# Sums into the state ahead of the gate, two later units for the third norm's tokens, and both ends of the MoE part rearranged

## The chip, the cores and the metric
The kernel is one program on one core of one Trainium2 chip. The metric is the time of one execution on the device in microseconds (us). The kernel before has a median of 2390.23 us over three runs (2389.24 to 2395.43).

## The reference
Two layers with four layer norms over 16 sequences of 512 tokens of width 128, all in f32. `P` is 128, and the batch number is called i, j or b below.

```
x = norm(x + ssm(x))            # W_in, causal conv of 4 taps, pointwise product, silu; 8 states:
                                #   h = exp(delta*A)*h + delta*B*u;  y = sum over states of C*h
                                #   y = (y + xc*D) * silu(z);  y @ W_out
x = norm(x + x @ sign(W).T)
x = norm(x + attn(x))           # 16 heads of 64:  s = exp(g)*s + k^T v;  o = q s,  k gated by sigmoid
                                #   RMS norm of o, gate sigmoid(x @ Wog.T), @ Wo.T
x = norm(x + moe(x))            # logits x @ gate; top 2 of 8 experts, softmax of the two
                                #   silu(x @ w0[e]) * (x @ w1[e]) @ wo[e], mixed by the two weights
```

## The kernel before, in words
The work falls into three parts. First come **rounds** (`rounds`, L562, a hardware loop over round r from 3 to 15 with the first and last rounds written out). A round does three things at once for three different batches: the front of the state-space model for batch n, its eight states and first two norms for batch i, and the attention of batch j. A round has eight **units** u (`project(u, j)`: products q, g and k of one pair of heads) and then eight **stages** h (`stage(h, i, j, n)`: chunk c = h // 2 of 128 tokens, half f = h % 2 of the heads). The third norm and the routing of batch j - 1 (`closing(u, j - 1, j)`) lie between the units. The order of every engine is the order in which the code is written; engines meet only at semaphores.

PE writes into six PSUM banks used in turn (`ring_uses`, `Uses`); a product waits until the bank's last reader has drained it. In a stage PE does `update` (bank U, the chunk's sum for the state), `front(h + 1)` (v, the gates, the turned keys, two masks D and two score banks S), some of the state-space products, every second stage `project_out`, and last `outputs(h)`. With seven or nine uses in a stage, a late bank of `front(h + 1)` is the one that held U, so PE waits there for DVE's `add_update(h)` (L1603; L1605 in the first chunk). DVE's `gate_out(h - 1)` (L1561, L1565) reads the outputs of the stage before, once ACT has squared them (L1163). The scans of the states (L1448), the products with C (L1456, `ch`) and with B (L1441, `push`) also run on DVE, and POOL adds each `ch` to `y` by a DMA that accumulates (L1875). POOL also raises variances to the power -0.5 (L1880).

The second part is the **turn**: the last batch's choice of experts, the rows' places (`find_rows`, POOL), the store of the rows by indirect DMA (`send_rows`, L1944), the zero rows behind each expert's region (`pad_rows`, L664, SP), the table of tiles (DVE, L1759 to L1777), and the first loads of rows (L680). Then 136 tiles of 128 rows go through the experts (L1016, L1027), and their results are scattered.

The third part is the **final norm**: for each batch SP loads the two results of each token (`load_both`, L697), POOL adds the token (`add_token`, L2027), DVE adds the two (L1833) and takes the statistics, POOL makes scale and shift, ACT normalizes (L1358), and SP stores (L701).

Of the kernel before, what the change touches and what calls it, by code (L numbers as in the profile page):

```python
# [7 lines left out]
P = 128  # L8
T = 512
TILES = T // P  # L10
# [7 lines left out]
EXPERTS = 8  # L18
# [16 lines left out]
LN_STEPS = 11  # L35
RMS_EPS = float(np.finfo(np.float32).eps)
# [165 lines left out]
LATE = {0: [f"wo_{TILES - 1}"], 3: ["x3T"], 4: ["route"]}  # L202
# [7 lines left out]
FINAL_SLOTS = 4  # L210

# [4 lines left out]
PRODUCTS_IN_UNIT = {2: 1, 4: 2, 6: 3}  # L216
# [11 lines left out]
INDEX_STAGE = 0  # L228
SPREAD_AFTER = {4: (2, 3), 7: (4, 5, 6, 7)}

def build(nc, a, out):
# [6 lines left out]
    with ExitStack() as ctx:  # L238
# [32 lines left out]
        minus_half = sb_kept("minus_half", [P, TILES])  # L271
# [11 lines left out]
        def sem(name):  # L283
# [114 lines left out]
        both = sb_kept("both", [P, FINAL_SLOTS, 2, TILES, P])  # L398
# [11 lines left out]
        x3_dram = nc.dram_tensor("x3_scratch", [B, T, P], F32, kind="Internal").ap().rearrange(  # L410
            "b (c p) d -> b p c d", p=P)
# [104 lines left out]
        s_both = [sem(f"both_results_loaded{n}") for n in range(FINAL_SLOTS)]  # L516
# [24 lines left out]
        out_dram = out.rearrange("b (c p) d -> b p c d", p=P)  # L541
        both_dram = results_dram[0:2 * B * T, :].rearrange("(r b c p) d -> r b p c d", r=2, b=B, p=P)
# [14 lines left out]
        HOT_STEPS, ROW_STEPS, SHARE_STEPS = 13, 14, 5  # L557
        STAGES = 2 * TILES
# [3 lines left out]
        def rounds(eng, body):  # L562
# [7 lines left out]
            body(None, B - 1, None)  # L570

# [7 lines left out]
        def _(sp):  # L579
# [93 lines left out]
            def load_rows(i):  # L673
                for n in range(2):
# [4 lines left out]
                    for c in range(MOE_LOAD):  # L679
                        sp.dma_start(rows_in[:, n, c, :], rows_dram[rows_at(g * MOE_LOAD + c), :]).then_inc(s_rows_in[n], 16)  # L680

            def load_tokens(b):
                sp.dma_start(tokens[:, bass.ds(b * TILES, TILES), :],
                             x3_dram[bass.ds(b, 1)].rearrange("b p c d -> (b p) c d")).then_inc(s_tokens, 16)
# [10 lines left out]
            def load_both(b):  # L695
                for r in range(2):
                    sp.dma_start(both[:, b % FINAL_SLOTS, r, :, :], both_dram[r, b]).then_inc(s_both[b % FINAL_SLOTS], 16)  # L697

# [1414 lines left out]
```

## Time and profile before
| | us |
|---|---|
| median of three runs | 2390.23 |
| the profiled execution, its own time | 2394.66 |
| its span | 2392.8 |
| PE busy in the span | 2069.4 (86%) |
| DVE busy | 1955.2 (82%) |
| ACT busy | 1411.5 (59%) |
| POOL busy | 838.3 (35%) |

The busy shares are averages over the three parts. The profile's slices show PE at 0.8 to 1.0 through the rounds and through the tiles, and at 0 in the last 60 us. The chain that ended last is PE for 50% of the span, DVE for 21%, issue for 12% and ACT for 9%. A row of a timeline gives the start in us, the length, the engine, the line and what it writes and reads; in brackets stands how long the engine was idle before, and what it waited for.

### The profile page before, as it was taken

The page shows a single profiled execution, that of the slowest core. Times are in us where ns is not written, and L with a number is a line of the kernel's source. Part 1 is how long each engine was busy: PE and PEld are TensorE (multiplying, and loading weights), DVE is VectorE, ACT ScalarE, POOL GpSimd, SP SyncE. Part 2 cuts the span into 40 slices and gives each one's busy share as a digit, 9 for nine tenths or more (in the row PEclk, how much of TensorE's full clock was granted, in tenths as well). Part 3 has the DMA queues.
Part 4 walks back from the last instruction along what each step waited for, and adds up shares of the span by engine and source line. Part 5 has one row for each costly group of instructions (what it writes and reads, how often), then busy time and mean ns, then how long its engine had stood idle before and what let it go on. Part 6 is the DMA issues. An engine that isn't in the chain of part 4 may idle for free.

```text
span 2392.8 us, 52303 instructions
## 1 busy us (share of the span) xinstructions
PE 2069.4 (86%) x15736; PEld 1543.1 (64%) x15865; DVE 1955.2 (82%) x3681; ACT 1411.5 (59%) x3240; POOL 838.3 (35%) x1060
## 2 busy tenths in 40 slices
PE   4589999998999898989898999989989569999980
PEld 2256666665656575756565665656676569999980
DVE  6788989889898989898989898888985457777768
ACT  3466676666766667676676666666656323333334
POOL 0011515152524343342514151515243233333337
PEclk7699999999999999999999999999999889999995
DMA  6352424334242434242515243333421232212216
GB/s 179 89 116 59 116 72 106 88 84 105 67 106 67 118 81 111 72 110 64 124 49 127 62 115 77 95 97 75 102 67 35 76 104 59 58 55 62 60 57 191
DMA packets 154382, 212.88 MB, mean 89 GB/s; under 512 B 20296, under 2 KB 88912, under 8 KB 153920
## 3 DMA queue, kind: packets, MB, share of 16 engines
q1 hardware_dynamic: 132048, 144.20, 20.5%
q0 software_dynamic: 22272, 67.92, 13.8%
q8 instruction: 31, 0.51, 0.1%
q14 instruction: 31, 0.25, 0.0%
HBM read 134.71 MB, written 28.08 MB: 68 GB/s over the span
## 4 chain that ended last, share of the span: by engine, by line
PE 50%; DVE 21%; issue 12%; ACT 9%; DMA 4%; POOL 1%; DVEq 1%; SPq 0%; ACTq 0%; POOLq 0%
PE banks L1016 8%; PE banks L1027 4%; PE banks L911 4%; PE banks L889 3%; PE banks L884 3%; DVE ch L1456 3%; PE banks L859 3%; PE banks L750 3%; PE banks L838 3%; PE banks L854 3%; PE banks L807 3%; DVE hs L1448 2%; DVE push L1441 2%; DMA y<-ch 2%; ACT S L1195 2%
## 5 line engine op out<-in xcount | busy, mean ns | idle before, releaser
L1448 DVE TENSOR_TENSOR_SCAN hs<-decay,push 128x512 f32<-128x512 f32 x256 | 312.9, 1244 | 4.9
L1195 ACT ACTIVATE S<-banks,fall_tok 128x128 f32<-128x128 f32 x1024 | 277.7, 384 | 27.3 <-PE banks L826 27.1
L1016 PE MATMUL banks<-rowsT,w_here 128*128 128x128 f32 x2176 | 269.2, 277 | 6.9 <-DVE w_here L1795 6.8
L1016 PEld LDWEIGHTS banks<-rowsT,w_here 128*128 128x128 f32 x2176 | 255.6, 193 | 10.5 <-issue 9.3
L1875 POOL DMA_DIRECT2D y<-ch x96 | 88.0, 917 | 451.2 <-DVE ch L1456 349.3
L1966 POOL TENSOR_TENSOR qd<-q,q_fall 128x512 f32<-128x512 f32 x96 | 157.9, 1645 | 239.5 <-ACT chunk_fall L1180 239.4
L2009 POOL DMA_INDIRECT results_scratch<-rows_out,result_to x136 | 131.9, 970 | 241.1 <-ACT rows_out L1323 234.3
L1554 DVE TENSOR_TENSOR S<-banks,S 128x512 f32<-128x512 f32 x256 | 166.5, 681 | 45.0 <-PE banks L838 26.7
L1441 DVE TENSOR_TENSOR push<-du,b_all 128x1024 f32<-128x1024 f32 x128 | 198.0, 1547 | 4.6 <-DMA b_all<-bc_scratch 4.6
L1312 ACT ACTIVATE tanh_h<-banks 128x512 f32<-128x512 f32 x136 | 81.3, 598 | 203.4 <-PE banks L1016 203.4
L838 PE MATMUL banks<-q,k 64*128 64x128 f32 x1024 | 152.0, 290 | 51.2 <-DVE state L1603 37.2
L1944 POOL DMA_INDIRECT rows_scratch<-x,row_now x128 | 172.0, 1344 | 40.2 <-issue 36.6
L1106 ACT ACTIVATE decay<-delta,a_neg 128x512 f32<-128x512 f32 x256 | 172.0, 730 | 20.2 <-DVE hs L1448 19.4
L1561 DVE SCALAR_TENSOR_TENSOR oT<-tog,banks 128x512 f32<-128x512 f32 x128 | 87.3, 682 | 106.1 <-ACT sq L1163 105.6
L807 PE MATMUL banks<-x2T,w_k 128*128 128x512 f32 x256 | 134.0, 605 | 45.5 <-DVE k L1547 45.5
L838 PEld LDWEIGHTS banks<-q,k 64*128 64x128 f32 x1024 | 127.5, 193 | 66.1 <-DVE state L1603 31.8
L1456 DVE TENSOR_TENSOR ch<-hs,c_all 128x1024 f32<-128x1024 f32 x128 | 159.9, 1249 | 3.1 <-DMA y<-ch 1.0
L1880 POOL TENSOR_TENSOR rstd<-var,minus_half 128x4 f32<-128x4 f32 x48 | 48.7, 1014 | 297.9 <-DVE var L1422 297.9
L839 PE MATMUL banks<-q,k 64*128 64x128 f32 x1024 | 152.5, 291 | 0.0
L911 PEld LDWEIGHTS banks<-w_o,oT 128*128 128x128 f32 x1024 | 123.6, 193 | 35.6 <-issue 33.5
L1163 ACT ACTIVATE sq<-banks 128x512 f32<-128x512 f32 x128 | 76.9, 601 | 116.3 <-PE banks L889 116.3
L1027 PE MATMUL banks<-w,act_h 128*128 x1088 | 143.6, 275 | 0.4 <-DVE act_h L1787 0.4
(218 smaller groups left out, 5139.2 us busy)
## 6 DMA issues: line engine op xcount, KB each, us to landing
y<-ch POOLq DMA_DIRECT2D x96, 512.0 KB, 5.4
b_all<-bc_scratch SPq DMA_DIRECT2D x128, 256.0 KB, 3.8
c_all<-bc_scratch SPq DMA_DIRECT2D x128, 256.0 KB, 3.6
q_fall<-fall_scratch SPq DMA_DIRECT2D x192, 128.0 KB, 3.3
rows_in<-rows_scratch SPq DMA_DIRECT2D x136, 66.0 KB
both<-results_scratch SPq DMA_DIRECT2D x32, 256.0 KB, 3.4
w<-w_dram SPq DMA_DIRECT2D x3, 2048.0 KB, 8.8
xT<-xT_dram SPq DMA_DIRECT2D x16, 256.0 KB, 2.9
```

The lines of the kernel that those rows point to most:

```text
L807: pe.matmul(bank, w[:, u * P:(u + 1) * P], x2T[:], start=True, stop=True).then_inc(full, 1)
L838: even = pe.matmul(low[:, at_h], k[0:DH, pair, here], q[0:DH, pair, here], start=True, stop=True)
L911: pe.matmul(bank[:, 0:P], oT[:, t, :], w_o[:, t, :], start=(t == 0), stop=(t == PAIRS - 1))
L1016: mm = pe.matmul(bank_h[:, u % 2, n, here], w_here[:, u % 2, n, here], x, start=True, stop=True)
L1027: mm = pe.matmul(bank_y[:, u % 2, 0:P], act_h[:, u % 4, f * P:(f + 1) * P], w_2[:, bass.ds(e * FF + f * P, P)], start=(f == 0), stop=(f == ...
L1106: nc.scalar.activation(decay[:, n % 2, h, :], delta[:, h, :], ACT.Exp, scale=a_neg[:, h, n:n + 1]).then_inc(s_decay, 1)
L1195: ins = nc.scalar.activation(S[:, g, here], bank[:, here], ACT.Exp, bias=fall_tok[:, head:head + 1])
L1441: nc.vector.tensor_tensor(push[:], du[:], b_all[:, slot, :].unsqueeze(1).broadcast_to([P, HALVES, T]), ALU.mult).then_inc(s_push, 1)
L1448: nc.vector.tensor_tensor_scan(hs[:, h, :], decay[:, n % 2, h, :], push[:, h, :], 0.0, ALU.mult, ALU.add).then_inc(s_scan, 1)
L1456: nc.vector.tensor_tensor(ch[:, n % 2, :, :], hs[:], c_all[:, slot, :].unsqueeze(1).broadcast_to([P, HALVES, T]), ALU.mult).then_inc(s_ch, 1)
L1554: nc.vector.tensor_tensor(S[:, g, :], full(ring, f"S{g}_{c}", j), S[:, g, :], ALU.mult).then_inc(ring.free_sem(f"S{g}_{c}"), 1)
L1944: nc.gpsimd.indirect_dma_start(out=rows_dram, out_offset=bass.IndirectOffsetOnAxis(ap=row_now[:, n, t:t + 1], axis=0), in_=x3_rows[:, t, : ...
```

## The change
It has four pieces.

1. In every stage from the third on, DVE adds the chunk's sum to the state (`add_update`) ahead of `gate_out`.
2. In the units, the products of state 1 (`ch` of state 1 and `push` of state 2) go from unit 2 to unit 1, those of state 2 from unit 4 to unit 3. PE turns the third norm's tokens in unit 4 instead of 3 and takes the logits in unit 5 instead of 4; DVE chooses the experts in unit 6, behind the seventh key, instead of in unit 5.
3. At the turn, the last batch's places are found on DVE (`find_last_rows`) in nine counted steps; the zero rows are split between SP and ACT; the row numbers of the first four tiles are read before the wait for the scattered rows; and the first weights are copied before the first rows are awaited.
4. In the final norm, tokens, results and output move with four consecutive tokens per partition (2 KB in one piece instead of four pieces of 512 bytes); `both` has eight slots instead of four; DVE adds the token, POOL no longer does; mean, variance, scale and shift are made for two batches at a time; and ACT issues the stores.

```diff
-LATE = {0: [f"wo_{TILES - 1}"], 3: ["x3T"], 4: ["route"]}
+LATE = {0: [f"wo_{TILES - 1}"], 4: ["x3T"], 5: ["route"]}
-PRODUCTS_IN_UNIT = {2: 1, 4: 2, 6: 3}
+PRODUCTS_IN_UNIT = {1: 1, 3: 2, 6: 3}
+CHOOSE_UNIT = 6
+BOTH_SLOTS = 8
@@ layouts
+        tokens_dram = x3_scratch.rearrange("b (p c) d -> b p c d", p=P)
-        out_dram = out.rearrange("b (c p) d -> b p c d", p=P)
-        both_dram = results_dram[0:2 * B * T, :].rearrange("(r b c p) d -> r b p c d", r=2, b=B, p=P)
+        out_dram = out.rearrange("b (p c) d -> b p c d", p=P)
+        both_dram = results_dram[0:2 * B * T, :].rearrange("(r b p c) d -> r b p c d", r=2, b=B, p=P)
@@ SP, turn
-            for e in range(EXPERTS):
-                pad = bass.ds(sp.value_load(pad_row[0:1, e:e + 1], min_val=0, max_val=ALL_ROWS - P), P)
-                sp.dma_start(rows_dram[pad, :], a["pad_rows"][e * P:(e + 1) * P, :]).then_inc(s_spared, 16)
+            clear_pads(sp, range(EXPERTS // 2))
             sp.wait_ge(s_tile_row, 1)
+            first_rows = [bass.ds(sp.value_load(row_i[0:1, c:c + 1], min_val=0, max_val=ALL_ROWS - P), P)
+                          for c in range(MOE_LOAD)]
             sp.wait_ge(s_spared, 16 * (EXPERTS + 1))
             sp.wait_ge(s_scattered, 16 * 2 * TOK_TILES)
@@ SP, end
-            for b in range(FINAL_SLOTS):
-                load_both(b)
             for b in range(B):
-                store(b, b % FINAL_SLOTS)
-                if b + FINAL_SLOTS < B:
-                    sp.wait_ge(s_mixed, b + 1)
-                    load_both(b + FINAL_SLOTS)
+                after(sp, s_mixed, b - BOTH_SLOTS + 1)
+                load_both(b)
@@ PE and ACT, closing: the two blocks move from u == 3 and u == 4
+                if u == 4:
+                    pe.wait_ge(s_x3, at(j, TILES, TILES))
...
+                if u == 5:
+                    bank, full = fill(ring, "route", it, "x3T")
@@ ACT
+            act.wait_ge(s_pads, 1)
+            clear_pads(act, range(EXPERTS // 2, EXPERTS))
...
+            def store(b):
+                n = b % FINAL_SLOTS
+                act.wait_ge(s_final, TILES * (b + 1))
+                act.dma_start(out_dram[b], final[:, n]).then_inc(s_out[n], 16)
             for b in range(B):
                 normalize_final(b)
+                if b:
+                    store(b - 1)
+            store(B - 1)
@@ DVE, stage
                 if j is not None:
-                    if h == 1:
-                        add_update(h, j)
+                    add_update(h, j)
                     if h:
                         gate_out(h - 1, j)
-                    if h != 1:
-                        add_update(h, j)
@@ DVE, turn
+            def find_last_rows(j):
...
+                for t in range(TILES):
+                    step(nc.vector.tensor_tensor(next_row[:, t + 1, :], next_row[:, t, :], ranks[:, 1, t, :], ALU.add))
+                nc.vector.tensor_copy(pad_row[:], done[0:1, :]).then_inc(s_pads, 1)
+                step(nc.vector.tensor_tensor(ranks[:, 0], ranks[:, 0], next_row[:, 0:TILES, :], ALU.add))
+                for n in range(2):
+                    step(nc.vector.tensor_tensor(rows_f[:], ranks[:, 0], hot[:, n], ALU.mult))
+                    step(nc.vector.tensor_reduce(row_f32[:, n, :], rows_f[:], AX.X, ALU.add))
@@ DVE, first tile
+            weights_here(0, 0)
             rows_to(0, 0)
@@ DVE, end
-            for b in range(B):
-                mix_results(b)
-                final_deviation(b)
+            dve.wait_ge(s_tokens, 16 * B)
+            for m in range(B // 2):
+                for step in (mix_results, add_token, final_stats):
+                    for b in (2 * m, 2 * m + 1):
+                        step(b)
+                final_deviation(m)
@@ POOL, body: sum_state(m, i) stands ahead of closing(u, ...), in the units of PRODUCTS_IN_UNIT
@@ POOL, end: add_token is gone
-            for b in range(B):
-                final_shift(b)
+            for m in range(B // 2):
+                final_shift(m)
```

The first place is DVE's row between the deviation of the third norm (`x3`, in unit 1) and the key of unit 3, in the loop. `hs` is the scan, `ch` and `push` the products of the states, `k` a key, `fall` the running sum of the decay. Before:

```order
L1547 SCALAR_TENSOR_TENSOR k<-tg,banks 128x512
L1429 TENSOR_SCALAR x3<-x3,mean,rstd 128x128 x4
L1526 SCALAR_TENSOR_TENSOR sp_in<-sp_in,sp_ln 112x512
L1533 SCALAR_TENSOR_TENSOR fall<-ones,sp_in 112x128 x4
L1456 TENSOR_TENSOR ch<-hs,c_all 128x1024
L1441 TENSOR_TENSOR push<-du,b_all 128x1024
L1448 SCALAR_TENSOR_TENSOR hs<-decay,push 128x512
L1448 SCALAR_TENSOR_TENSOR hs<-decay,push 128x512
L1547 SCALAR_TENSOR_TENSOR k<-tg,banks 128x512
```

Now:

```order
L1476 TENSOR_TENSOR ch<-hs,c_all 128x1024
L1461 TENSOR_TENSOR push<-du,b_all 128x1024
L1567 SCALAR_TENSOR_TENSOR k<-tg,banks 128x512
L1449 TENSOR_SCALAR x3<-x3,mean,rstd 128x128 x4
L1546 SCALAR_TENSOR_TENSOR sp_in<-sp_in,sp_ln 112x512
L1553 SCALAR_TENSOR_TENSOR fall<-ones,sp_in 112x128 x4
L1468 SCALAR_TENSOR_TENSOR hs<-decay,push 128x512
L1468 SCALAR_TENSOR_TENSOR hs<-decay,push 128x512
L1567 SCALAR_TENSOR_TENSOR k<-tg,banks 128x512
```

The products of state 1 and the push of state 2 stand before the key and the normalizing of `x3`, where they stood behind the decay's sums; the scan of state 2 no longer follows its push directly.

On POOL, at the same place, `rms` and `rstd` belong to the third norm and `y<-ch` is the accumulating DMA of a state. Before:

```order
L1886 TENSOR_TENSOR rms<-mixed,rms_eps 128x1
L1889 TENSOR_TENSOR rms<-rms,minus_half 128x1
L1880 TENSOR_TENSOR rstd<-var,minus_half 128x4
L1875 DMA y<-ch 128x1024
L1875 DMA y<-ch 128x1024
L1875 DMA y<-ch 128x1024
```

Now:

```order
L1941 TENSOR_TENSOR rms<-mixed,rms_eps 128x1
L1944 TENSOR_TENSOR rms<-rms,minus_halves 128x1
L1930 DMA y<-ch 128x1024
L1935 TENSOR_TENSOR rstd<-var,minus_halves 128x4
L1930 DMA y<-ch 128x1024
L1930 DMA y<-ch 128x1024
```

The DMA of state 1 is issued ahead of the norm's power, where it came behind it.

On DVE in stage 2, `oT` and `sq_less` are the gate of stage 1's outputs and `state` the chunk's sum. Before:

```order
L1481 SCALAR_TENSOR_TENSOR xc<-th,xc 128x512
L1561 SCALAR_TENSOR_TENSOR oT<-tog,banks 128x512
L1565 TENSOR_TENSOR sq_less<-sq 128x256
L1603 TENSOR_TENSOR state<-state,banks 64x4x64 x2
L1448 SCALAR_TENSOR_TENSOR hs<-decay,push 128x512
L1587 TENSOR_TENSOR kd<-banks,to_end 128x512
```

Now:

```order
L1501 SCALAR_TENSOR_TENSOR xc<-th,xc 128x512
L1623 TENSOR_TENSOR state<-state,banks 64x4x64 x2
L1581 SCALAR_TENSOR_TENSOR oT<-tog,banks 128x512
L1585 TENSOR_TENSOR sq_less<-sq 128x256
L1468 SCALAR_TENSOR_TENSOR hs<-decay,push 128x512
L1607 TENSOR_TENSOR kd<-banks,to_end 128x512
```

The two halves of the sum stand ahead of the two instructions of the gate; nothing is added.

## Rows read from the trace of the kernel before

**Rows 1.** Windows view of one middle round: stretch, busy us per engine, clock, DMA.
```profile
1008.87:1121.62 112.75, 102.96 (x770) 71.21 (x778) 98.77 (x178) 77.02 (x180) 41.82 (x50) 1.00 0.37 90
```

**Rows 2.** Line L1113 over the whole span: durations in ns, first and last start.
```profile
L1113 ACT COPY x2T<-banks x16: 585/586/586, 103.0 to 1796.1; 128x512 f32<-128x512 f32 x16
```

**Rows 3.** Waits of PE, whole span: who waited for whom, us, times, longest.
```profile
PE banks L807 <- DVE k L1547: 45.5, 29, 2.7
PE banks L838 <- DVE state L1603: 37.2, 16, 4.6
...
PE banks L956 <- DVE x L1429: 20.3, 16, 5.7
...
PE banks L743 <- DVE state L1603: 6.8, 14, 0.5
```

**Rows 4.** Timeline of DVE, projections of that round: start us, length, then idle before.
```profile
1022.86 0.69 DVE L1547 SCALAR_TENSOR_TENSOR k<-tg,banks 128x512 f32<-128x512 f32 x1 [0.69 <-ACT tg L1141]
1023.46 1.11 DVE L1429 TENSOR_SCALAR x<-x,mean,rstd 128x128 f32<-128x128 f32 x4
...
1026.66 1.20 DVE L1456 TENSOR_TENSOR ch<-hs,c_all 128x1024 f32<-128x1024 f32 x1
1027.77 1.22 DVE L1441 TENSOR_TENSOR push<-du,b_all 128x1024 f32<-128x1024 f32 x1
1029.12 2.34 DVE L1448 TENSOR_TENSOR_SCAN hs<-decay,push 128x512 f32<-128x512 f32 x2
```

**Rows 5.** Timeline of POOL, the same stretch.
```profile
1022.24 1.02 POOL L1880 TENSOR_TENSOR rstd<-var,minus_half 128x4 f32<-128x4 f32 x1 [4.95 <-DVE var L1422]
1028.45 0.92 POOL L1875 DMA_DIRECT2D y<-ch  x1 [5.20 <-DVE ch L1456]
```

**Rows 6.** Timeline of DVE in stage 2 of that round.
```profile
1066.37 0.67 DVE L1561 SCALAR_TENSOR_TENSOR oT<-tog,banks 128x512 f32<-128x512 f32 x1
...
1067.31 0.86 DVE L1603 TENSOR_TENSOR state<-state,banks 64x256 f32<-64x256 f32 x2
```

**Rows 7.** Timeline of PE in stage 2, the row that waits.
```profile
1068.22 0.37 PE L838 MATMUL banks<-q,k 64*128 64x128 f32 x1 [2.28 <-DVE state L1603]
```

**Rows 8.** Timeline of ACT in stage 4, the row that starts its long chain.
```profile
1096.27 0.69 ACT L1090 ACTIVATE delta<-banks,b_dt 128x512 f32<-128x512 f32 x1 [1.56 <-PE banks L769]
```

**Rows 9.** Line L1944 at the turn, 1895 to 1930 us.
```profile
L1944 POOL DMA_INDIRECT rows_scratch<-x,row_now x8: 954/978/1855, 1910.5 to 1920.5; - x8
```

**Rows 10.** Line L1699 at the turn, 1895 to 1910 us.
```profile
L1699 DVE TENSOR_TENSOR hot<-hot,rev x2: 191/192/192, 1900.7 to 1902.1; 128x32 f32<-128x32 f32 x2
```

**Rows 11.** Timeline of all engines from the last ranks to the first expert product.
```profile
1903.71 1.03 POOL L1909 TENSOR_TENSOR next_row<-next_row,ranks 128x8 f32<-128x8 f32 x4 [8.84 <-ACT ranks L1259]
...
1923.86 8.49 SPq L680 DMA_DIRECT2D rows_in<-rows_scratch  x8
...
1929.63 0.16 DVE L1801 TENSOR_TENSOR is_best<-rows_in,expert_place 128x4 f32<-128x4 f32 x1 [11.51 <-DMA rows_in<-rows_scratch]
...
1930.84 0.58 ACT L1306 COPY rowsT<-banks 128x512 f32<-128x512 f32 x1 [27.19 <-PE banks L1002]
...
1932.78 1.62 PE L1016 MATMUL banks<-rowsT,w_here 128*128 128x128 f32 x6 [2.05 <-DVE w_here L1795]
```

**Rows 12.** Line L1833, the final sum on DVE, whole span.
```profile
L1833 DVE TENSOR_TENSOR final_in<-both x16: 683/692/694, 2332.5 to 2384.4; 128x512 f32<-128x512 f32 x16
```

**Rows 13.** Timeline of all engines in the final norm.
```profile
2334.63 1.28 POOL L2027 TENSOR_TENSOR both<-both,tokens 128x512 f32<-128x512 f32 x1 [2.15 <-DMA both<-results_scratch]
...
2368.89 1.23 DVE L1844 TENSOR_TENSOR var<-stats 128x4 f32<-128x4 f32 x1
...
2371.24 0.87 DVE L1839 BATCH_NORM_STATS2 stats<-final_in 128x6 f32<-128x128 f32 x4
...
2388.34 1.65 ACT L1358 ACTIVATE final<-final_in,shift,rstd 128x128 f32<-128x128 f32 x4 [0.41 <-POOL shift L2036]
```

**Rows 14.** Windows view, ten us in the middle of the final norm.
```profile
2355.00:2365.00 10.00, 0.00 (x0) 0.00 (x0) 9.59 (x36) 4.94 (x12) 8.12 (x8) 0.50 0.80 224
```

More of the change, by code:

```diff
@@ L397, in build @@
         rows_out = sb_kept("rows_out", [P, 2, MOE_LOAD, P])
-        both = sb_kept("both", [P, FINAL_SLOTS, 2, TILES, P])
+        both = sb_kept("both", [P, BOTH_SLOTS, 2, TILES, P])
         stats4 = sb_kept("stats4", [P, FINAL_SLOTS, TILES, 6])
@@ L515, in build @@
         s_results = [sem("results_stored0"), sem("results_stored1")]
-        s_both = [sem(f"both_results_loaded{n}") for n in range(FINAL_SLOTS)]
+        s_both = [sem(f"both_results_loaded{n}") for n in range(BOTH_SLOTS)]
         s_mixed = sem("results_mixed")
@@ L557, in build, with last @@
         HOT_STEPS, ROW_STEPS, SHARE_STEPS = 13, 14, 5
+        LAST_ROW_STEPS = 9
+        def last(j):
+            return isinstance(j, int) and j == B - 1
         STAGES = 2 * TILES
@@ L570, in rounds, with clear_pads @@
             body(None, B - 1, None)
+        def clear_pads(eng, some):
+            for e in some:
+                pad = bass.ds(eng.value_load(pad_row[0:1, e:e + 1], min_val=0, max_val=ALL_ROWS - P), P)
+                eng.dma_start(rows_dram[pad, :], a["pad_rows"][e * P:(e + 1) * P, :]).then_inc(s_spared, 16)
         def attention_over(eng):
@@ L1725, in body @@
                             fall_less(FALL_PARTS.index(u), j)
+                        if u == CHOOSE_UNIT and not first(j):
+                            choose(j - 1, j)
                     if i is not None and u in PRODUCTS_IN_UNIT:
@@ L1740, in _, with step @@
                 closing(u, B - 1, END)
+                if u == CHOOSE_UNIT:
+                    choose(B - 1, END)
+            attention_over(dve)
+            done = next_row[:, TILES, :]
+            def find_last_rows(j):
+                steps = [0]
+                def step(ins):
+                    steps[0] += 1
+                    ins.then_inc(s_route, 1)
+                    dve.wait_ge(s_route, at(j, ROW_STEPS, steps[0]))
+                drained(dve, ring, END, "rank")
+                dve.wait_ge(s_route, at(j, ROW_STEPS, 0))
+                dve.wait_ge(s_row_now, at(j, 3, 0))
+                for t in range(TILES):
[5 more added lines that the diff above has]
+                    step(nc.vector.tensor_reduce(row_f32[:, n, :], rows_f[:], AX.X, ALU.add))
+                assert steps[0] == LAST_ROW_STEPS
+            find_last_rows(B - 1)
             index_rows(B - 1)
-            attention_over(dve)
-            dve.wait_ge(s_route, ROW_STEPS * B)
-            done = next_row[:, TILES, :]
-            nc.vector.tensor_copy(pad_row[:], done[0:1, :]).then_inc(s_pads, 1)
             steps = [0]
@@ L1811, in experts @@
                     t = i * MOE_BODY + u
-                    weights_here(t, u)
+                    if u or not first(i):
+                        weights_here(t, u)
                     if u == MOE_LOAD - 1:
@@ L1938, in send_rows @@
                     pool.wait_ge(s_share, at(j, SHARE_STEPS, SHARE_STEPS))
-                    nc.gpsimd.tensor_tensor(next_row[:, 0, :], next_row[:, TILES - 1, :], ranks[:, 1, TILES - 1, :],
-                                            ALU.add).then_inc(s_route, 1)
+                    if not last(j):
+                        nc.gpsimd.tensor_tensor(next_row[:, 0, :], next_row[:, TILES - 1, :], ranks[:, 1, TILES - 1, :],
+                                                ALU.add).then_inc(s_route, 1)
                 for k in SCATTERS[u]:
@@ L1953, in closing @@
                 if u == RANK:
-                    find_rows(j, it)
+                    if not last(j):
+                        find_rows(j, it)
                     shares(j)
```

88 lines of the change are left out of this document (41 added, 47 removed).

## The prediction
> **What bounds the kernel now.** I read the page first: span, shares, slices and the chain that ended last. PE is on that chain for half of it, so the next view is who PE waits for; then one middle round of the timeline, engine by engine; last the turn from the rounds to the experts and the final norm, where PE is idle. The reader is to see four things.
>
> A round takes (1796.1 - 103.0) / 15 = 112.9 us [rows 2]. In the one I followed PE is busy for 102.96 of 112.75 us and DVE for 98.77 [rows 1]: neither is full, they take turns in waiting. PE's waits are for DVE nearly all: for a key's bank 45.5 us in all, for the chunk's sum 37.2 us in 16 waits (and 6.8 us at another bank), for the third norm's tokens 20.3 us in 16 [rows 3]. The round's clock is 1.00, the upper of TensorE's two levels (2.4 GHz) [rows 1], so those waits don't lower it. At the turn PE does nothing from the last ranks to 1929.63. In the final norm DVE is busy for 9.59 of 10 us [rows 14], but 1.23 us of that is an instruction on 128x4 elements that lay beside POOL's token sum [rows 13]; an instruction of that size beside an idle POOL takes 0.16 [rows 11].
>
> **Sums ahead of the gate.** Nothing is added; two DVE instructions of the gate go behind two of the sum. In stage 2 the gate starts at 1066.37 and the sum at 1067.31 [rows 6], so the sum comes 0.94 us earlier. PE stood idle for 2.28 us for it [rows 7], so it gets the whole 0.94. The table has 16 such waits of 2.3 us on average [rows 3], one to a round: 16 x 0.94 = 15.0 us. The gate is now 0.86 us later. Who waits for it: `project_out`, which PE reaches only behind a convolution or the mix, and ACT's gates in the stages where a new pair of chunks begins; I cost that at nothing, and if the cover were missing it would cost up to the 0.86 in one stage of each round.
> The 6.8 us at the other bank, in stage 5, will go too, but I count nothing for them: by then the round hangs on ACT. ACT's step sizes start when PE's L769 is done (1.56 us idle before, [rows 8]) and run through exp and log into the masks that DVE needs, and the next round's `push` follows from there. L769 lies behind stage 2 and ahead of stage 5, so the 0.94 us passes through it and the 0.5 us doesn't. Bounds: 0 (given back at another wait) and 15.0 + 6.8 = 21.8.
>
> **The units.** PE's wait for the third norm's tokens (about 0.95 us a round) goes, as it asks a unit later. That is worth nothing by itself: PE next waits for the keys anyway [rows 3], and those hang on DVE's row. So I count DVE's stalls. Before, the key of unit 2 had 0.69 us of idle time ahead of it, and the normalizing followed at once [rows 4]. Now ch of state 1 starts at about 1022.1, where the deviation ends, and takes 1.20. POOL must issue its DMA before the power: in [rows 4, 5] the DMA starts 0.59 behind the end of ch and takes 0.92, and the power takes 1.02; 1022.1 + 1.2 + 0.6 + 0.9 + 1.0 = 1025.8. DVE meanwhile has ch, push and the key (1.11, 1.22 and 0.60 by the starts and lengths of [rows 4]), done at 1025.0: a new stall of 0.8 in place of 0.69. Against it, a push is no longer followed at once by the scan that reads it, which cost 0.13 of idle each (1027.77 + 1.22 to 1029.12, [rows 4]), twice a round, and the second split of the decay no longer waits for ACT's cast, an estimate of 0.15 by the same kind of gap. Sum -0.8 + 0.69 + 0.4 = 0.3 us a round, 14 rounds: 4.2 us. Bounds: a gain of 1.2 a round if the power isn't delayed at all (17), and a loss of 1.0 a round (14), if the power is stretched beside push as far as that line's neighbours are, 1.0 and more.
> The choice of experts does the same work one key later; nothing waits for it before PE's ranks, behind front(0).
>
> **The turn.** POOL begins the places at 1903.71 [rows 11] and the first scatter starts at 1910.5 [rows 9], 6.8 us later. Now DVE takes ten counted or plain small steps of 0.225 (six of them in 1902.1 - 1900.7, [rows 10]), then three small instructions (0.36, two of them without a wait) and the scatter's own start (0.3, estimates both), and POOL's shares run beside it: scatter at 2.9 us. Gain 3.9; the eight scatters keep their ten us. The zero rows start at about 1904.7 on two queues and are out of the way. Behind the scatters SP reads a row number ahead of each load: eight loads in 8.49 us, 1.06 apart; the first four rows have landed 5.77 us after the first issue [rows 11]. With the numbers read before, the issues are, as an estimate, 0.43 apart: 3 x 0.63 = 1.9 us less. The first product started 1.36 us behind the turned rows (1930.84 + 0.58 to 1932.78), held by the weights' copy; with that copy ahead, 0.1: gain 1.2. Sum 7.0. Bounds 3 (the scatters' landing or the 2 MB weight loads hold it) and 9.
>
> **The final norm.** DVE's period is (2384.4 - 2332.5) / 15 = 3.46 us a batch [rows 12]. Without the stretched instruction (1.23 to 0.16, [rows 13]) a deviation is 3.46 - 0.72 - 0.87 - 1.07 = 0.8. A pair is now four sums of 0.69, two statistics of 0.87, one deviation of 0.8 and 0.1 of gaps: 5.4 us in place of 6.92. ACT has 2 x 1.65 [rows 13] and two stores to issue, 0.4 each as an estimate, 4.1 a pair, and keeps up, but a pair's second sum waits for the batch four before, and that loop (4.5 on DVE, 2.3 on POOL, 3.8 on ACT for two pairs) gives 5.3: just covered. The start: pair 0 needs the second batch, landed at 2334.63 before [rows 13], in longer pieces perhaps 2333.0; DVE is done with it at 2337.7, with the last pair at 2375.5. Then power and shift on eight columns 2.0, ACT 1.65 + 0.4 + 1.65, two stores, and the 2.8 us from ACT's end (2388.34 + 1.65) to the span's: 2384.4. Gain 8.4. Bounds 4 (loads as slow as before, the loop 0.4 longer) and 11.
>
> In this stage the DMA moved 224 GB/s at a share of 0.80 [rows 14], 280 GB/s when full; a pair moves 1.57 MB, which is 5.6 us at that rate, about DVE's 5.4. The Trainium skill (DMA: Bandwidth & Descriptors, Specifications) says that transfers from 512 bytes up already run at line rate. By that rule the longer pieces bring nothing, the pair would take 5.6 and the second batch would land as before: the end would gain 8.4 - 1.4 - 1.6 = 5.4, and the total below would be 31.6 in place of 34.6. No row here shows the same stream in 2 KB pieces, so this stays open; the range holds both.
>
> **Sum.** 15.0 + 4.2 + 7.0 + 8.4 = 34.6 us. The profiled execution has 2394.66 us, 1.9 more than its span and 4.4 more than the median: 2394.66 - 34.6 = 2360.1 for one like it, and 2390.23 - 34.6 = 2355.6 against the median. I say 2355.
>
> **Rivals.**
> - Only the ends gain. For it: PE waits 45.5 us for keys [rows 3], and what it gains at the sum's bank can be given back there, since DVE's own row in stage 2 gets no shorter. Against it: the start of ACT's chain follows PE. 2390.2 - 15.4 = 2374.8.
> - The rounds gain more: the power isn't delayed (17), the other bank's 6.8 us count as well: 21.8 + 17 + 15.4 = 54: 2336.
> - Slower: POOL's DMA in front of the power. It waits for ch of state 1 and for the start of the sum, so the normalizing of x3, behind it the decay, the scan of state 2 and every key after it stand still, on DVE, which has 14 us to spare in a round. It decides when the new stall exceeds 0.8 + 34.6 / 14 = 3.3 us a round. At 5 us it costs 14 x 4.2 = 59: 2390.2 - 34.6 + 59 = 2414. Against it: the 0.92 and 1.02 us of [rows 5].
> - Ends and rounds cancel: each round loses about 1 us, the bound above: 2390.2 - 15.4 + 14 = 2389.
> - The change doesn't do what it says: it is described as bringing state 1's product a unit later, but the table moves it from unit 2 to unit 1, earlier, and DVE's row shows this. The sums above go by the row, so no chance of its own.
>
> **How the numbers follow.** Forecast 0.52, only the ends 0.22, more in the rounds 0.15, cancelled 0.06, slower 0.05. What this kernel's measurement can tell from no change is about 0.3%, 7 us: below 2383 is faster. Faster 0.52 + 0.22 + 0.15 = 0.89, same 0.06, slower 0.05. The range leaves out the last two and the far end of the third case: 2332 to 2377. The forecast's own is 2345 to 2365.
>
> **What would show it.** The distance between x2T copies falls from 112.9 to about 111.6. PE's wait for L838 at the chunk's sum falls from 2.3 to about 1.4 us each, the one at the turned x1 goes to 0, and that for the third norm's tokens vanishes; a new wait of DVE appears at the normalizing of x3, for the power, near 0.8 us. The first scatter starts 2.9 us behind the ranks, the first product 3.8 + 1.9 us behind the first row load's issue. The last stage has one deviation per 5.4 us and ends 8 us sooner. I am wrong if the round's length doesn't fall (the key waits grow by what the sum's waits lose), if the stall at x3 is over 2 us, or if the two-batch loop through ACT, not DVE, sets the final norm at 6 us or more.

## The result, and the profile after

The changed kernel has a median of 2362.35 us over four runs (2360.64 to 2369.59), the kernel before 2392.83 over four; the ratio of the two is 0.9876, with a 95% interval of 0.9844 to 0.9907. The prediction was 2355 us, range 2332 to 2377. The profiled execution took 2363.93 us, span 2362.1: 30.7 us less than the one before, where the terms summed to 34.6. The total is close; two of its four terms are not, and they have opposite signs. One of the six executions of the kernel with the power first (experiment 2) took 5701.25 us; it counts in that kernel's median of 2344.79, but not in its ratio.

First the rounds. This is the line that copies x2T, once a round:

```profile
L1122 ACT COPY x2T<-banks x16: 586/586/586, 106.1 to 1785.1; 128x512 f32<-128x512 f32 x16
```

From the first to the last that is 1679.0 us in place of 1693.1 [rows 2]: 111.9 a round, 0.94 less, where 1.24 were predicted. The first copy comes 3.1 us later (106.1 for 103.0); in the twelve kernels of the experiments it lies between 102.8 and 106.2, whether they have the change or not, so I take that as scatter. The next view is the windows view of whole rounds (stretch, its length, busy us and instructions of PE, PE's weight loads, DVE, ACT, POOL, then PE's clock, DMA share, GB/s). The clock's column is the granted clock as a share of full speed. Two rounds of the kernel before, and five us inside the second:

```profile
1008.90:1121.60 112.70, 102.96 (x770) 71.21 (x778) 98.72 (x178) 76.97 (x179) 41.82 (x50) 1.00 0.37 90
1121.60:1235.90 114.30, 104.49 (x770) 71.79 (x778) 99.38 (x178) 77.07 (x181) 41.03 (x50) 0.99 0.36 91
1181.60:1186.60 5.00, 5.00 (x19) 2.31 (x18) 4.97 (x7) 1.36 (x3) 4.39 (x4) 0.66 0.12 41
```

Two rounds of the changed kernel, and six us inside the second:

```profile
776.20:887.90 111.70, 102.97 (x770) 71.02 (x778) 98.00 (x177) 76.92 (x180) 41.85 (x50) 1.00 0.38 92
1001.20:1114.30 113.10, 106.00 (x770) 72.84 (x778) 98.33 (x177) 77.17 (x180) 41.07 (x50) 0.97 0.34 89
1025.20:1031.20 6.00, 6.00 (x14) 3.39 (x13) 6.00 (x8) 4.20 (x8) 0.92 (x1) 0.50 0.71 187
```

The column of the clock is what the prediction missed. In both kernels there are rounds at 1.00 and rounds in which the clock falls to the lower of its two levels (0.50) for some us, and those are longer on average. Over the 13 rounds from the second copy to the fifteenth:

| | rounds with a fall | where | us a round at full clock | us with a fall | all 13 |
|---|---|---|---|---|---|
| before | 6 | 60 us in, stage 2 | 112.9 | 114.2 | 1475.2 |
| changed | 10 | 24 us in, units | 111.2 | 112.9 | 1462.7 |

What PE did before each fall stands in its timeline. Before, in the units and stage 2 of the second round; the last is the wait of [rows 7], a round later:

```profile
1144.97 1.12 PE L807 MATMUL banks<-x2T,w_k 128*128 128x512 f32 x2 [1.62 <-DVE k L1547]
...
1152.26 1.12 PE L807 MATMUL banks<-x2T,w_k 128*128 128x512 f32 x2 [1.47 <-DVE k L1547]
...
1181.09 0.37 PE L838 MATMUL banks<-q,k 64*128 64x128 f32 x1 [2.27 <-DVE state L1603]
```

In the changed kernel, units and stage 2 of the second round:

```profile
1019.79 0.66 PE L965 MATMUL banks<-eye,x 128*128 128x128 f32 x4 [0.87 <-DVE x L1449]
1024.77 1.67 PE L816 MATMUL banks<-x2T,w_k 128*128 128x512 f32 x2 [2.61 <-DVE k L1567]
...
1061.79 0.34 PE L847 MATMUL banks<-q,k 64*128 64x128 f32 x1 [1.52 <-DVE state L1623]
```

The wait for the chunk's sum is 1.52 in place of 2.27, and the clock no longer falls behind it. But PE stands idle for 2.61 us in one piece for the key of unit 3, where it had 1.62 and 1.47 in two pieces 7 us apart, and now the clock falls there. The matmuls behind it show it: a projection of two matmuls takes 1.67 to 2.05 us in place of 1.02. The Trainium skill (TensorE: Matmul & The Clock Gate, A second HAM failure mode: psum-queue depth-cycling) tells of a kernel in which short idle pieces of PE between groups of matmuls made its clock swing between the two levels. The trace agrees in so far as the clock falls here in 10 of 13 rounds, though PE is busy for 106.00 of the 113.1 us of the round shown; but here the falls stand behind one long piece and not behind many short ones.

PE's waits, 212.1 to 1674.8 us (who waited for whom, us, times, longest); these answer to [rows 3], which are of the whole span:

```profile
PE banks L816 <- DVE k L1567: 37.5, 22, 2.6
...
PE banks L965 <- DVE x L1449: 11.0, 13, 0.9
```

DVE's row in the units, to be held against [rows 4]:

```profile
1014.78 1.23 DVE L1476 TENSOR_TENSOR ch<-hs,c_all 128x1024 f32<-128x1024 f32 x1
...
1017.06 0.68 DVE L1567 SCALAR_TENSOR_TENSOR k<-tg,banks 128x512 f32<-128x512 f32 x1
1018.62 1.11 DVE L1449 TENSOR_SCALAR x<-x,mean,rstd 128x128 f32<-128x128 f32 x4 [0.88 <-POOL rstd L1935]
...
1021.83 2.31 DVE L1468 TENSOR_TENSOR_SCAN hs<-decay,push 128x512 f32<-128x512 f32 x2
1024.06 0.66 DVE L1567 SCALAR_TENSOR_TENSOR k<-tg,banks 128x512 f32<-128x512 f32 x1
```

and POOL's, against [rows 5]:

```profile
1016.60 0.91 POOL L1930 DMA_DIRECT2D y<-ch  x1 [6.60 <-DVE ch L1476]
1017.26 1.33 POOL L1935 TENSOR_TENSOR rstd<-var,minus_halves 128x4 f32<-128x4 f32 x1
```

POOL issues state 1's DMA ahead of the power, DVE waits 0.88 us for the power (0.8 was predicted), and the scan of state 2 comes before the next key: from one key to the next 7.0 us. In stage 2 DVE's order is the planned one, against [rows 6]:

```profile
1060.78 0.86 DVE L1623 TENSOR_TENSOR state<-state,banks 64x256 f32<-64x256 f32 x2
1061.67 0.69 DVE L1581 SCALAR_TENSOR_TENSOR oT<-tog,banks 128x512 f32<-128x512 f32 x1
```

Then the turn, against [rows 9] and [rows 11]:

```profile
1892.98 0.78 DVE L1777 TENSOR_TENSOR next_row<-next_row,ranks 128x8 f32<-128x8 f32 x4 [0.70 <-ACT ranks L1268]
...
1895.81 1.07 POOL L2000 DMA_INDIRECT rows_scratch<-x,row_now  x1 [0.80 <-DVE x L1690]
...
1908.91 6.70 SPq L697 DMA_DIRECT2D rows_in<-rows_scratch  x8
...
1912.38 0.16 DVE L1840 TENSOR_TENSOR is_best<-rows_in,expert_place 128x4 f32<-128x4 f32 x1 [3.57 <-DMA rows_in<-rows_scratch]
...
1914.25 2.08 PE L1025 MATMUL banks<-rowsT,w_here 128*128 128x128 f32 x8 [0.68 <-ACT rowsT L1318]
```

First scatter 2.8 us behind the start of the places (6.8 before; 2.9 predicted), first rows used 3.5 us behind the first load's issue (5.8; 3.8 predicted), first product 1.9 us behind that (3.15; 1.9 predicted). And the final norm, against [rows 12] and [rows 13]:

```profile
L1874 DVE TENSOR_TENSOR final_in<-both x16: 684/692/693, 2311.2 to 2349.9; 128x512 f32<-128x512 f32 x16
```

and the second sum of one pair of batches and of the next:

```profile
2329.10 0.69 DVE L1874 TENSOR_TENSOR final_in<-both 128x512 f32<-128x512 f32 x1 [0.19 <-ACT final L1370]
...
2334.30 0.69 DVE L1874 TENSOR_TENSOR final_in<-both 128x512 f32<-128x512 f32 x1 [0.20 <-ACT final L1370]
```

A pair takes 5.2 us (2334.3 - 2329.10; 5.4 predicted), the first load to the span's end 54.3 us in place of 65.4.

### The profile page after: what moved, and what is told of

Its sections match the earlier page's. It is cut to its first block and busy times, and to the rows that moved or that the text cites. A ratio compares the mean times of both kernels' runs of the same rounds, so it can differ in the third digit from the quotient of the medians.

```text
span 2362.1 us, 52250 instructions
## 1 busy us (share of the span) xinstructions
PE 2090.2 (88%) x15736; PEld 1555.9 (66%) x15865; DVE 1930.9 (82%) x3650; ACT 1411.8 (60%) x3240; POOL 810.2 (34%) x1014
## 3 DMA queue, kind: packets, MB, share of 16 engines
q1 hardware_dynamic: 105040, 139.73, 19.9%
## 5 line engine op out<-in xcount | busy, mean ns | idle before, releaser
L847 PE MATMUL banks<-q,k 64*128 64x128 f32 x1024 | 147.3, 284 | 39.3 <-DVE state L1623 25.2
L816 PE MATMUL banks<-x2T,w_k 128*128 128x512 f32 x256 | 142.9, 641 | 42.3 <-DVE k L1567 42.2
L848 PE MATMUL banks<-q,k 64*128 64x128 f32 x1024 | 147.9, 285 | 0.0
L816 PE MATMUL banks<-x2T,w_q 128*128 128x512 f32 x256 | 144.8, 649 | 0.0
L863 PE MATMUL banks<-w_v,x2T 128*128 128x512 f32 x256 | 143.3, 641 | 0.0
```

Of the source, the lines that this page charges most:

```text
L816: pe.matmul(bank, w[:, u * P:(u + 1) * P], x2T[:], start=True, stop=True).then_inc(full, 1)
L847: even = pe.matmul(low[:, at_h], k[0:DH, pair, here], q[0:DH, pair, here], start=True, stop=True)
```

## Experiments

Each of these kernels was timed beside the kernel before, in 4 to 12 executions, and its ratio is to those. Rounds, falls and waits are read from one profiled execution of each. Theory P is the prediction: every term is a sum of work and of waits. Theory C, formed after the result, adds the clock: it falls behind a stretch in which PE does little, and a change is also worth what it does to those stretches.

### 1. The four pieces, each alone

Each is the kernel before with one of the four numbered pieces of the change and nothing else. The whole edit of the first, and the core of the second:

```diff
                 if j is not None:
-                    if h == 1:
-                        add_update(h, j)
+                    add_update(h, j)
                     if h:
                         gate_out(h - 1, j)
-                    if h != 1:
-                        add_update(h, j)
```

```diff
-LATE = {0: [f"wo_{TILES - 1}"], 3: ["x3T"], 4: ["route"]}
+LATE = {0: [f"wo_{TILES - 1}"], 4: ["x3T"], 5: ["route"]}
-PRODUCTS_IN_UNIT = {2: 1, 4: 2, 6: 3}
+PRODUCTS_IN_UNIT = {1: 1, 3: 2, 6: 3}
+CHOOSE_UNIT = 6
```

> The kernel before with only the chunk's sums put ahead of the gate. Theory P (the prediction's terms): each round 0.94 us shorter, 15 to 16 us in all, ratio 0.9935. Theory C (the granted clock counts as well): PE's wait of 2.3 us in stage 2 falls to 1.4, so the clock no longer falls 58 to 66 us into a round, as it did in 6 of 13 middle rounds of the kernel before (114.1 us with the fall, 112.7 without), and the two copies' waits add up: the middle rounds take 111 to 111.3 us, all at 1.00; 13 x 2.3 = 30 us, ratio 0.987. Rival N: what is gained at the sum is given back at the keys; ratio 1.000, and the wait for keys grows from 40 us.

> The kernel before with only the units changed (products of states 1 and 2 a unit earlier, x3 turned in unit 4, logits in 5, choice behind the seventh key). Theory P: 4 us faster, ratio 0.998. Theory C: DVE waits 0.9 us for POOL's power ahead of the normalizing of x3, PE then waits 2.6 us in one piece for the key of unit 3, and the clock falls 22 to 32 us into the round in most rounds; the first state copy comes 41.2 us into the round in place of 38.7. Middle rounds 114.5 to 116 us, slower by 10 to 25 us, ratio 1.004 to 1.010. Rival N: same within 0.1%.

> The kernel before with only the final norm changed (four tokens per partition, eight slots, sums on DVE, two batches a deviation, stores by ACT). Theory P: 8.4 us faster, ratio 0.9965. By the trace of the changed kernel, where the first load of both results to the span's end took 54.3 us in place of 65.4: 11.1 us faster, ratio 0.9954. Rival: the gain there came from an earlier landing that this kernel does not have; under 5 us.

> The kernel before with only the turn changed (places on DVE in nine steps, zero rows on two queues, row numbers read ahead, first weights copied ahead). Theory P: 7.0 us faster, ratio 0.997. By the trace of the changed kernel, where last ranks to the first load of both results took 8.8 us less: ratio 0.9963. Rival: the tiles are held by the weight loads and give it back; under 2 us.

| alone | median us | ratio, interval | us by the ratio | predicted |
|---|---|---|---|---|
| sums | 2366.93 | 0.9886 (0.9870 to 0.9903) | -27 | -15.0 |
| units | 2421.32 | 1.0111 (1.0094 to 1.0128) | +27 | -4.2 |
| final norm | 2385.78 | 0.9961 (0.9943 to 0.9978) | -9 | -8.4 |
| turn | 2383.03 | 0.9959 (0.9945 to 0.9972) | -10 | -7.0 |

Theory C has the signs of the first two and nearly their sizes: 0.987 and 1.004 to 1.010 were expected. It had not expected the second fall with the units alone. A round with the sums alone, and PE's wait for the chunk's sum in it:

```profile
992.60:1104.10 111.50, 103.13 (x778) 71.18 (x778) 98.52 (x177) 76.90 (x179) 41.85 (x50) 1.00 0.37 94
```

```profile
1051.59 0.37 PE L838 MATMUL banks<-q,k 64*128 64x128 f32 x1 [1.34 <-DVE state L1603]
```

A round with the units alone, and its two falls:

```profile
1023.80:1139.60 115.80, 107.86 (x778) 73.87 (x778) 99.34 (x178) 77.30 (x180) 40.17 (x50) 0.96 0.34 89
1046.00:1054.00 8.00, 7.08 (x15) 3.88 (x16) 7.76 (x10) 5.38 (x11) 0.92 (x1) 0.60 0.63 158
1082.00:1096.00 14.00, 11.54 (x87) 8.55 (x87) 11.77 (x14) 6.71 (x19) 9.29 (x8) 0.88 0.50 124
```

and what PE waited for ahead of them:

```profile
1046.92 1.42 PE L808 MATMUL banks<-x2T,w_k 128*128 128x512 f32 x2 [2.61 <-DVE k L1548]
...
1084.87 0.34 PE L839 MATMUL banks<-q,k 64*128 64x128 f32 x1 [2.46 <-DVE state L1604]
```

With the sums alone the 13 rounds take 1447.2 us, and the clock fell in one of them, behind a wait of 2.08 us for the third norm's tokens. With the units alone they take 1502.3, and the clock fell twice in every one: behind 2.6 us of waiting for the key and behind 2.5 for the sum. The two parts of the ends were as predicted. The product of the four ratios is 0.992, not 0.988: the units cost less where the sums are also early. In the changed kernel no second fall is left in the 13 rounds, which fits.

The granted clock averaged over a whole execution is known for every one that was timed, and it goes the same way: 0.953 to 0.961 before, 0.946 to 0.950 changed, 0.959 to 0.960 with the sums alone, 0.934 to 0.938 with the units alone, 0.963 to 0.965 in the kernel with the old units below. So the falls are not a matter of the profiled executions only.

### 2. The units taken back, and POOL's power put first

The first is the changed kernel with the units as before (the second diff above backwards). The second changes POOL's body only:

```diff
-                    if m is not None:
+                    if m is not None and u != 1:
                         sum_state(m, i)
                     if j is not None:
                         if not first(j):
                             closing(u, j - 1, j)
+                    if m is not None and u == 1:
+                        sum_state(m, i)
```

> The changed kernel with the units as before (products of states 1 and 2 in units 2 and 4, x3 turned in unit 3, logits in 4, choice ahead of the seventh key). Theory C: middle rounds as with the sums alone, 111.2 us at 1.00, 16 us less than the changed kernel; ratio to before 0.981. Theory P: the units' 4 us are lost; ratio 0.989. Rival: the three gains overlap; 0.987.

> The changed kernel with POOL's power for x3 put ahead of the accumulating DMA of state 1 in unit 1. Theory C: DVE's wait of 0.9 us ahead of the normalizing of x3 goes, PE's wait for the key of unit 3 falls from 2.6 to 1.7 us in one piece, the clock stays at 1.00 in the units, and the middle rounds take 110.4 to 111.2 us in place of 112.5: 17 to 27 us less than the changed kernel, ratio to before 0.977 to 0.981. Theory P (no effect of the clock): 0.9 us a round at most, 12 us, ratio 0.983. Rival: PE gets the wait back at the next key; ratio 0.987 as the changed kernel.

Old units: 2346.58 us, ratio 0.9804 (0.9784 to 0.9824); all 13 rounds at 1.00, 111.4 us each, 1447.9 in all. So the new units cost the changed kernel 0.9876 - 0.9804, some 17 us; 14.8 of it lies in these 13 rounds. The product of the other three ratios is 0.981, so those gains add up. Between rounds at full clock they are worth next to nothing (111.2, of only three such rounds, to 111.4): the loss goes with the falls of the clock.

Power first: 2344.79 us, ratio 0.9786 (0.9764 to 0.9808), as expected in its size but not in its way. DVE's waits for the power, in the 13 rounds of the changed kernel:

```profile
DVE x L1449 <- POOL rstd L1935: 26.3, 26, 1.1
```

and of this one:

```profile
DVE x L1449 <- POOL rstd L1935: 14.7, 13, 1.1
```

The 0.9 a round went, and so did PE's wait for x3. PE's wait for the key did not shrink: PE came to it as much earlier as DVE did, and here is what is left of it:

```profile
PE banks L816 <- DVE k L1567: 36.2, 17, 2.6
```

The pieces are still of 2.6 us, and the clock still fell in 12 of 13 rounds. What came was 11.1 us in the 13 rounds (1451.6), near the stall of 0.88 times 13. But two more rounds had a fall, and the one round without took 109.5 us, 1.8 less than such rounds of the changed kernel, so that agreement is in part chance. In the profiled executions the last x2T copy comes 19.9 us earlier, at 1765.2: 3.3 us of it stand before the first copy and 5.4 behind the fifteenth, where the changed kernel's clock fell twice and this one's once.

### 3. More work for PE

The same matmuls are done three times over, so that PE reaches its long wait later; nothing else changes:

```diff
-                    for t in range(TILES):
+                    for t in 3 * list(range(TILES)):
                         mm = pe.transpose(bank[:, t * P:(t + 1) * P], x3[:, t, :], eye[:])
```

> The changed kernel with more work on PE: the four transposes of x3 are done three times over into the same bank, about 1.0 us more of PE ahead of its wait for the key of unit 3. If the fall of the clock follows from the piece of 2.6 us in which PE is idle, that piece shrinks to about 1.6 us, the clock stays at 1.00 and the kernel with more work is faster: middle rounds 111.2 to 111.8 us, 10 to 17 us less than the changed kernel, ratio 0.981 to 0.983. If it does not, the rounds are as long as in the changed kernel or up to 1 us longer: ratio 0.987 to 0.993.

> The changed kernel with POOL's power first and the four transposes of x3 done three times over: 1.0 us more of PE work ahead of its longest wait. Theory C: the piece in which PE is idle falls from 2.6 to 1.6 us, the clock falls in few rounds, middle rounds 109.5 to 110.8 us, 11 to 28 us less than with the power alone; ratio 0.967 to 0.974. Without an effect of the clock: 0.9786 or up to 0.984.

PE in the units of a round with the extra work alone, then that round and one with a fall:

```profile
1125.92 1.53 PE L965 MATMUL banks<-eye,x 128*128 128x128 f32 x12 [0.88 <-DVE x L1449]
1130.91 1.12 PE L816 MATMUL banks<-x2T,w_k 128*128 128x512 f32 x2 [1.74 <-DVE k L1567]
```

```profile
1107.20:1218.20 111.00, 103.84 (x778) 71.89 (x786) 98.09 (x178) 76.79 (x180) 41.84 (x50) 1.00 0.37 93
546.40:659.40 113.00, 106.85 (x778) 73.66 (x786) 98.98 (x178) 77.07 (x180) 41.04 (x50) 0.97 0.36 92
```

The changed kernel with 0.9 us more work a round is faster: 2350.60 us, ratio 0.9806 (0.9784 to 0.9828), against 0.9876 (0.9844 to 0.9907) without it. The kernel of experiment 5, which has the changed kernel's rounds and was timed beside this one, has 0.9877. Its wait is 1.74 in place of 2.61, and the clock fell in 6 of 13 rounds in place of 10. With the power first as well it is 2333.17 us, ratio 0.9747 (0.9729 to 0.9766), the fastest of all kernels here, though short of the 0.967 to 0.974 expected; the 13 rounds take 1438.3, and 9 of them were at 1.00. No sum of work and waits gives that sign: the wait is shorter by just the work that was added. It is an experiment and no good way to write a kernel: real work should stand there.

### 4. Real work or another order in its place

```diff
-SCANS_IN_UNIT = {1: 1, 3: 2, 5: 3}
-PRODUCTS_IN_UNIT = {1: 1, 3: 2, 6: 3}
+SCANS_IN_UNIT = {1: 1, 4: 2, 6: 3}
+PRODUCTS_IN_UNIT = {1: 1, 4: 2, 6: 3}
```

with the power first (even keys); the same with the products of state 3 in unit 7; and the even keys with the logits in unit 6 and the choice in unit 7.

> The changed kernel with POOL's power first, and state 2's scan and products moved from unit 3 to unit 4 and state 3's scan from unit 5 to 6, so that DVE's keys of units 3, 4 and 5 stand 3 to 4 us apart (5.4 and 2.9 between the keys of units 2, 3 and 4 with the power alone). Theory C: no piece of PE's wait for a key exceeds 1.7 us, the clock stays at 1.00 in the units and the middle rounds take 109.5 to 110.5 us, 15 to 28 us less than with the power alone; ratio to before 0.967 to 0.973. Theory P (only DVE's and PE's sums of work and waits count): as with the power alone, 0.9786. Rival: DVE's later scans delay the states in the stages by up to 2 us a round; 0.98 to 0.99.

> As the kernel with the keys evenly apart, and state 3's products in unit 7 in place of 6, behind the last key. Theory C: the last key comes 2.4 us earlier; if PE waits for it, rounds up to 1 us shorter than with the even keys alone, and POOL's accumulating DMA of state 3 comes at the same time as before; ratio 0.963 to 0.973. Rival: same as with the even keys, within 0.1%.

> As the kernel with the even keys (POOL's power first, scans of states 2 and 3 in units 4 and 6, products of state 2 in unit 4), where PE waited 2.1 us in one piece ahead of the logits for ACT's copy of the turned x3 (13 times, 27.7 us) and the clock fell in every middle round. Here the logits come a unit later (6) and the choice behind the eighth key (unit 7), so that three projections lie between the turned tokens and the logits. Theory C: PE's longest piece of waiting in the units is under 1 us, the clock stays at 1.00 there, and the middle rounds take 109 to 110.3 us in place of 112.2: 25 to 40 us less than with the even keys, ratio to before 0.965 to 0.971. Theory P (waits alone): 2.1 us of PE's wait goes, but DVE and ACT have their row as before: up to 1 us a round, ratio 0.977 to 0.982. Rival: ACT, which stands 5.4 us at the running sum of the decay, holds PE at the next bank for as long; ratio 0.982.

All three missed: 2349.51 us (ratio 0.9819, 0.9797 to 0.9841), 2349.04 (0.9815, 0.9799 to 0.9831) and 2355.15 (0.9838, 0.9817 to 0.9859), where theory C expected 0.963 to 0.973. The second came out as its rival said, the same as the first. The 13 rounds take 1458.8, 1458.4 and 1458.0 us, 7 more than with the power alone. The waits show where the clock fell. PE in the units of the kernel with even keys:

```profile
1012.97 1.12 PE L816 MATMUL banks<-x2T,w_k 128*128 128x512 f32 x2 [0.47 <-DVE k L1567]
...
1016.75 1.12 PE L816 MATMUL banks<-x2T,w_k 128*128 128x512 f32 x2 [0.38 <-DVE k L1567]
1020.00 1.77 PE L970 MATMUL banks<-w_route,S 128*128 128x8 f32 x8 [2.13 <-ACT S L1150]
```

PE in the last one, then a round of it without a fall, one with, and six us in the second:

```profile
1016.99 1.12 PE L816 MATMUL banks<-x2T,w_k 128*128 128x512 f32 x2 [0.74 <-DVE k L1567]
1028.72 0.19 PE L978 MATMUL banks<-hot_bf,earlier 128*128 128x32 bf16 x1 [1.51 <-DVE hot_bf L1721]
1029.82 1.01 PE L910 MATMUL banks<-v,kd 128*64 128x64 f32 x16 [0.88 <-DVE kd L1607]
```

```profile
882.00:992.20 110.20, 103.32 (x778) 71.07 (x778) 97.66 (x177) 76.62 (x179) 40.16 (x50) 1.00 0.36 91
992.20:1104.80 112.60, 105.27 (x779) 71.95 (x778) 98.71 (x178) 76.79 (x181) 41.02 (x50) 0.98 0.36 94
1029.00:1035.00 6.00, 5.18 (x29) 3.72 (x30) 3.94 (x6) 1.64 (x5) 4.42 (x16) 0.72 0.50 110
```

With even keys PE waits under 0.5 us for each, runs ahead, and then stands 2.13 us in front of the logits for ACT's copy of the turned x3, which lies in ACT's row behind its wait for the decay's running sum; the clock fell in 13 of 13. With the logits later that is gone and no fall is left in the units; PE now waits for the choice (1.51 us, at the ranks) and for kd (0.88) with 0.2 us of work between them, and the clock fell behind them, 37 to 39 us into the round, in 11 of 13. Its rounds without a fall took 110.3, those with one 112.5. The idle time of PE had only moved, and each time a fall stood behind it. Nor is it the length of one wait alone: pieces of 1.62 us in the kernel before and in the one with the sums were followed by no fall in any round, 1.74 with the extra work in 6 of 13, and 1.51 and 0.88 close together in 11 of 13. What exactly decides stays open.

### 5. Pieces of 512 bytes

The changed kernel with its three layouts of the end as before:

```diff
-        tokens_dram = x3_scratch.rearrange("b (p c) d -> b p c d", p=P)
+        tokens_dram = x3_scratch.rearrange("b (c p) d -> b p c d", p=P)
...
-        both_dram = results_dram[0:2 * B * T, :].rearrange("(r b p c) d -> r b p c d", r=2, b=B, p=P)
+        both_dram = results_dram[0:2 * B * T, :].rearrange("(r b c p) d -> r b p c d", r=2, b=B, p=P)
```

> The changed kernel with tokens, results and output moved in pieces of 512 bytes again (token c * 128 + p on partition p), all else as in it. By the prediction's bound for the DMA the last stage gets 3 us longer (both-load start to end 57.3 in place of 54.3, the pair of batches 5.6 in place of 5.2); if pieces of 512 bytes move as fast as pieces of 2 KB, the same within 0.5 us. If the loads are slower still, 5.4 us a pair becomes 6 or more and the end 10 us longer.

DVE's sum over the whole stage:

```profile
L1874 DVE TENSOR_TENSOR final_in<-both x16: 684/692/693, 2313.0 to 2351.7; 128x512 f32<-128x512 f32 x16
```

The issues of the loads of both results, then the 40 us from the first of them, in the changed kernel:

```profile
2307.80 22.90 SPq L715 DMA_DIRECT2D both<-results_scratch  x32
2307.80:2347.80 40.00, 0.00 (x0) 0.00 (x0) 32.94 (x125) 17.01 (x43) 15.34 (x12) 0.51 0.75 271
```

and in this one:

```profile
2309.07 28.99 SPq L715 DMA_DIRECT2D both<-results_scratch  x32
2309.10:2349.10 40.00, 0.00 (x0) 0.00 (x0) 32.48 (x123) 16.55 (x42) 15.33 (x12) 0.51 1.01 269
```

2364.88 us, ratio 0.9877 (0.9858 to 0.9896), the same as with 2 KB. First to last sum on DVE is 38.7 us in both, so the transfers did not bound this stage. The prediction had weighed the rule of the Trainium skill (DMA: Bandwidth & Descriptors, Specifications) that transfers from 512 bytes up already run at line rate. In the kernel's time the trace agrees: the longer pieces bring nothing. In the transfers themselves it does not. For the same GB/s the engines' time in packets is a share of 1.01 with 512 bytes and 0.75 with 2 KB (a share over 1 means that packets overlap), and the 32 loads are issued over 28.99 us in place of 22.90. DVE's row and the eight slots hide it; what a stage bound by its transfers would gain, no run here shows. The gain of the end is that of the other edits to it, DVE's row and the slots, which were not taken apart.

## Why the prediction was right in its sum and wrong in two terms

The total in range is in good part luck. By the ratios the sums brought 12 us more than predicted, the units in this kernel 21 less (a cost of 17 for a gain of 4.2), the turn 3 and the end 1 more. That is 29 in sum, 30 by the ratio of the whole, where 34.6 were predicted: two misses cancel for the greater part. The expected 2355 itself was missed by 7 us.

- **Sums ahead of the gate, 15.0 predicted, 27 alone.** The step "so it gets the whole 0.94" holds: with the sums alone PE's wait fell from 2.27 to 1.34 us. The 0.5 us a round at the other bank, which I counted at nothing, came too: a round at full clock is 1.6 us shorter (112.9 to 111.3), 21 in 13 rounds. The other 7 of the 28 us in these rounds go with the clock: 6 rounds with a fall became one. In the changed kernel itself the wait only fell to 1.52.
- **What failed: "The round's clock is 1.00 [...] so those waits don't lower it."** I had read the clock of one round of 15, one without a fall. A windows view of every round would have shown 0.99 in six of the 13 middle ones, with rounds 1.3 us longer. The experiments then showed that PE's longest idle pieces have a price beside their length, and that a change that joins two of them can be dear.
- **The units, a gain of 4.2 predicted, a cost of 17 in this kernel, 27 alone.** The stall at the normalizing was 0.88 as worked out (0.8), and the rest of the sum came out as well: at full clock the units are worth 0.2 us a round (0.3 predicted), by the three such rounds of the changed kernel. The step that failed is again the clock: DVE's row put the power's wait, the normalizing, the decay and a scan between two keys, PE's waits of 1.62 and 1.47 became one of 2.61, and the 10 of 13 rounds with a fall are 1.7 us longer. PE's wait for x3 did not vanish (11.0 us in 13 rounds, 12.9 before): it asked 3 us later in the round, and the tokens came 3 us later too, behind the products and the power.
- **Turn, 7.0 predicted, 10 by the ratio (7 to 13).** The profile gives 7.8 from the places to the first product, by 4.0, 2.3 and 1.3 (3.9, 1.9 and 1.2 predicted) and 0.3 between them, and one us more in the tiles, which stays open.
- **Final norm, 8.4 predicted, 9 by the ratio (5 to 14), 11.1 in the profile.** The period was 5.2 for 5.4, and the last power, shift and store took 7.8 us from DVE's end in place of 8.9.
- **The rivals.** That a slower change could come through POOL's DMA ahead of the power had the right place and the wrong price: the stall stayed at 0.9, far below the 3.3 from which it was to decide, and yet the units lost. That the longer pieces bring nothing is true of the kernel's time; the end gained none the less.

The fastest version that the experiments point to without added work is the power first, or the old units, 22 and 17 us below the changed kernel by their ratios; their intervals overlap.

## What to carry to other kernels

Read TensorE's clock for every repetition of a loop, not for one, and note what PE did before each fall. Price a term that moves PE's waits twice: by their length at full clock, and by whether idle pieces are joined or split. When a piece of PE's waiting is removed, look for the place where it stands next; three rearrangements here only moved it.

## What was not expected of the hardware

- Falls of the clock to 0.50 for 3 to 7 us behind waits of 1.7 to 2.6 us inside rounds in which PE is over 90% busy. In the kernels with rounds of both kinds, those with a fall are 0.8 to 2.4 us longer on average (1.3 before, 1.7 changed). The same wait is not always followed by one (2.27 us before: 6 of 13 rounds; 2.61 us after: 10 of 13), so single runs and single rounds say little.
- The power on 128x4 elements on POOL took 1.93 us beside DVE's `ch` in the kernel with the power first and 1.33 beside `push` in the changed one; 1.02 in [rows 5].
- The same bytes take the DMA engines a share of 1.01 of their time in pieces of 512 bytes and 0.75 in pieces of 2 KB (experiment 5).
